# Inverse roots by a seed, a scaled Newton step and a third-order step, in 24 short VectorE chains of a graph and expert kernel

## The reference

```python
def _layernorm(x, axis=-1, eps=1e-05):
    m = jnp.mean(x, axis=axis, keepdims=True)
    v = jnp.var(x, axis=axis, keepdims=True)
    return (x - m) / jnp.sqrt(v + eps)
...
    x = x + _L0_gnn_ref(_layernorm(x, axis=-1), adj, L0_gnn_Wq, L0_gnn_Wk)
    x = x + _L0_ffn_ref(_layernorm(x, axis=-1)[None], ...)[0]
    x = x + _L1_gnn_ref(_layernorm(x, axis=-1), adj, 4096, L1_gnn_W, L1_gnn_b, L1_gnn_a)
    x = x + _L1_ffn_ref(_layernorm(x, axis=-1)[None], ...)[0]
```

## Time and profile before

| what | value |
|---|---|
| time, three runs | 826.5, 825.47, 826.3 us; median 826.3 us |
| span of the profiled execution | 825.4 us; the page gives no other time for it |
| instructions in the profile | 11636 |
| TensorE busy | 724.0 us, 88% of the span, x3481 |
| VectorE busy | 576.9 us, 70%, x1717 |
| ScalarE busy | 509.5 us, 62%, x774 |
| GpSimd busy | 180.4 us, 22%, x216 |
| stages, from the timeline | prepare to 68, attend to 449, mix and project to 547, gather and route to 825 us |

### The profile page before, as it was taken

How to read it: one execution, slowest core, us unless ns; L and a number is a source line. 1 busy time by engine, 2 the same in 40 slices (tenths; PEclk the granted TensorE clock), 3 DMA queues, 4 the chain that set the end, 5 groups by cost and what they waited for, 6 DMA issues and landing times. The chain is left out here.

```text
span 825.4 us, 11636 instructions
## 1 busy us (share of the span) xinstructions
PE 724.0 (88%) x3481; PEld 425.5 (52%) x3481; DVE 576.9 (70%) x1717; ACT 509.5 (62%) x774; POOL 180.4 (22%) x216
## 2 busy tenths in 40 slices
PE   1857999999999999999993799759999999779992
PEld 1643444444444444444442699535445656568871
DVE  7875667878787887878786458964666655655546
ACT  1736888888888888888883786841323443424330
POOL 2340000000000000000000444200445456646570
PEclk9969999999999999999997799879999999969997
DMA  4206999989997888778771200040002122124008
GB/s 130 81 0 189 316 284 253 286 255 290 259 274 230 252 229 257 238 230 259 217 218 47 95 1 2 0 116 13 27 30 70 57 69 74 42 78 107 24 27 280
DMA packets 97934, 121.92 MB, mean 148 GB/s; under 512 B 8510, under 2 KB 76355, under 8 KB 97616
## 3 DMA queue, kind: packets, MB, share of 16 engines
q1 hardware_dynamic: 93840, 113.72, 47.7%
q0 software_dynamic: 4032, 7.47, 2.8%
HBM read 87.47 MB, written 34.60 MB: 148 GB/s over the span
## 5 line engine op out<-in xcount | busy, mean ns | idle before, releaser
L562 DVE SCALAR_TENSOR_TENSOR probs<-adj,probs 128x1024 f32<-128x1024 int32 x128 | 156.7, 1224 | 77.5 <-ACT probs L535 68.4
L485 PE MATMUL ps<-x,qT 128*128 128x512 f16 x768 | 188.0, 382 | 3.2 <-PEq L203 3.2
L535 ACT ACTIVATE probs<-ps 128x1024 f32<-128x1024 f32 x128 | 130.9, 1023 | 51.1 <-PE ps L485 51.1
L546 ACT ACTIVATE mask<-probs 128x1024 fp8e4<-128x1024 f32 x128 | 134.0, 1047 | 0.0
L497 PE MATMUL ps<-probs,v 128*128 128x512 f32 x256 | 130.7, 592 | 0.0
L1462 PE MATMUL ps<-mask,parts 128*128 128x512 fp8e4 x512 | 119.7, 384 | 8.4 <-DVE parts L1829 8.4
L485 PEld LDWEIGHTS ps<-x,qT 128*128 128x128 f16 x768 | 75.5, 98 | 94.8 <-issue 5.6
L568 DVE TENSOR_TENSOR p_lo<-probs,p_hi 128x512 f16<-128x512 f32 x128 | 87.5, 684 | 0.1
L785 POOL MEMSET hT<- 128x128 f32 x1 | 0.2, 204 | 378.9 <-POOLq L438 378.9
L1462 PEld LDWEIGHTS ps<-mask,parts 128*128 128x128 f16 x512 | 50.1, 100 | 61.1 <-DVE parts L1829 8.5
L1789 POOL DMA_INDIRECT mixed_spill<-mask x70 | 68.8, 983 | 54.8 <-issue 28.2
(11 more groups left out here) (303 smaller groups left out, 1032.6 us busy)
## 6 DMA issues: line engine op xcount, KB each, us to landing
adj<-in_adj SPq DMA_DIRECT2D x128, 512.0 KB, 4.4
sorted_rows_spill<-blank SPq DMA_DIRECT2D x32, 528.0 KB
sorted_rows_spill<-blank SPq DMA_DIRECT2D x14, 330.0 KB
mask<-sorted_rows_spill SPq DMA_DIRECT2D x35, 132.0 KB, 2.3
mask<-mixed_spill SPq DMA_DIRECT2D x7, 512.0 KB, 7.8
mask<-in_x SPq DMA_DIRECT2D x4, 512.0 KB, 6.2
feat_spill<-mask SPq DMA_DIRECT2D x8, 256.0 KB, 2.0
x_feat<-in_x SPq DMA_DIRECT2D x8, 256.0 KB, 4.3
```

What stands on the lines that cost most here:

```text
L485: ins = nc.tensor.matmul(out, qT[:, q_half, j], kT[:, c, k_half * GROUP:(k_half + 1) * GROUP], start=(n == 0), stop=(n == 2))
L535: nc.scalar.activation(probs[:, k % RING, :], ps[:, b:b + 2, :].rearrange("p b n -> p (b n)"), ACT.Exp, scale=1.0 / QK_SCALE ** 2).then_in ...
L546: nc.scalar.activation(mask[:, k * W:(k + 1) * W], probs[:, k % RING, :], ACT.Sign, saturate=False).then_inc(mask_kept, 1)
L562: nc.vector.scalar_tensor_tensor(out=probs[:, k % RING, :], in0=adj[:, k % LOADS, :], scalar=0.0, in1=probs[:, k % RING, :], op0=ALU.is_gt ...
```

## The change

Each inverse root is computed in another way, from the negative variance. Epsilon and the scales of the results are taken into constants of instructions that are there anyway. Helper functions:

```diff
     me, mo, ve, vo = (stats[:, :, i] for i in (1, 4, 2, 5))
     ch.mark(nc.vector.tensor_tensor(mean, me, mo, ALU.add))
     ch.mark(nc.vector.tensor_tensor(t0, me, mo, ALU.subtract))
-    ch.link(nc.vector.tensor_tensor(t1, ve, vo, ALU.add))
-    ch.mark(nc.vector.tensor_scalar(mean, mean, 0.5, None, ALU.mult))
+    ch.link(nc.vector.scalar_tensor_tensor(out=t1, in0=ve, scalar=D * LN_EPS, in1=vo, op0=ALU.add, op1=ALU.add))
+    ch.mark(nc.vector.scalar_tensor_tensor(out=mean, in0=mean, scalar=-0.5, in1=mean, op0=ALU.mult, op1=ALU.add))
     ch.link(nc.vector.scalar_tensor_tensor(out=t0, in0=t0, scalar=0.25, in1=t0, op0=ALU.mult, op1=ALU.mult))
-    ch.link(nc.vector.scalar_tensor_tensor(out=var, in0=t1, scalar=1.0 / D, in1=t0, op0=ALU.mult, op1=ALU.add))
-
-
-def seed_root(nc, ch, y, v, t1):
-
-    ch.mark(nc.vector.tensor_scalar(y.bitcast(I32), v.bitcast(I32), -0.5, float(0x5F3759DF), ALU.mult, ALU.add))
-    ch.link(nc.vector.tensor_scalar(t1, v, -0.5, None, ALU.mult))
-
-
-def refine_root(nc, ch, y, t0, t1):
-
-    ch.link(nc.vector.tensor_tensor(t0, t1, y, ALU.mult))
-    ch.link(nc.vector.tensor_tensor(t0, t0, y, ALU.mult))
-    ch.link(nc.vector.scalar_tensor_tensor(out=y, in0=t0, scalar=1.5, in1=y, op0=ALU.add, op1=ALU.mult))
-
-
-def inverse_root(nc, ch, y, v, t0, t1):
-
-    seed_root(nc, ch, y, v, t1)
-    for _ in range(3):
-        refine_root(nc, ch, y, t0, t1)
+    ch.link(nc.vector.scalar_tensor_tensor(out=var, in0=t1, scalar=-1.0 / D, in1=t0, op0=ALU.mult, op1=ALU.subtract))
+
+
+def first_root(nc, ch, y, v, t0):
+
+
+    ch.link(nc.vector.tensor_scalar(y.bitcast(I32), v.bitcast(I32), -0.5, float(0x5F3759DF - 0x40000000), ALU.mult, ALU.add))
+    ch.link(nc.vector.tensor_tensor(t0, y, y, ALU.mult))
+    ch.link(nc.vector.tensor_tensor(t0, v, t0, ALU.mult))
+    ch.link(nc.vector.scalar_tensor_tensor(out=y, in0=t0, scalar=3.0, in1=y, op0=ALU.add, op1=ALU.mult))
+
+
+def last_root(nc, ch, y, v, t0, scale=1.0):
+
+
+    a, s = 0.5 * 1.000875, 0.375 * 0.5 * 1.000875 * scale
+    r = math.sqrt(s)
+    ch.link(nc.vector.scalar_tensor_tensor(out=t0, in0=y, scalar=-a * a * r, in1=y, op0=ALU.mult, op1=ALU.mult))
+    ch.link(nc.vector.tensor_tensor(t0, v, t0, ALU.mult))
+    ch.link(nc.vector.scalar_tensor_tensor(out=t0, in0=t0, scalar=-10.0 / 3.0 * r, in1=t0, op0=ALU.add, op1=ALU.mult))
+    ch.link(nc.vector.scalar_tensor_tensor(out=y, in0=t0, scalar=5.0 * s, in1=y, op0=ALU.add, op1=ALU.mult))
+
+
+def inverse_root(nc, ch, y, v, t0, scale=1.0):
+
+    first_root(nc, ch, y, v, t0)
+    last_root(nc, ch, y, v, t0, scale)
```

Stage 1, statistics and norms:

```diff
                 row_statistics(nc, ch, stats, mean[:, :], var[:, :], t0[:, :], t1[:, :])
-                ch.link(nc.vector.tensor_scalar(var[:, :], var[:, :], LN_EPS, None, ALU.add))
-                inverse_root(nc, ch, rstd[:, :], var[:, :], t0[:, :], t1[:, :])
-
-                ch.link(nc.vector.tensor_scalar(rstd[:, :], rstd[:, :], V_SCALE, None, ALU.mult))
+                inverse_root(nc, ch, rstd[:, :], var[:, :], t0[:, :], V_SCALE)
...
-                ch.link(nc.vector.tensor_scalar(ss[:, :], ss[:, :], 1e-8 * V_SCALE ** 2, None, ALU.max))
-                inverse_root(nc, ch, rnorm[:, :], ss[:, :], t2[:, :], t3[:, :])
-                nc.vector.tensor_scalar(rnorm[:, :], rnorm[:, :], QK_SCALE, None, ALU.mult).then_inc(norms_ready, 1)
-                dve.wait_ge(norms_ready, 1)
+                ch.link(nc.vector.tensor_scalar(ss[:, :], ss[:, :], 1e-8 * V_SCALE ** 2, -1.0, ALU.max, ALU.mult))
+                inverse_root(nc, ch, rnorm[:, :], ss[:, :], t2[:, :], QK_SCALE)
+                dve.sem_inc(norms_ready, 1)
```

Stage 2, the pieces of an ending (stages 3 and 4 drop their epsilon instruction, L928 and L1857, in the same way; ENDING goes from 33 to 29 and STEPS from 18 to 14):

```diff
                         row_statistics(nc, ch, sb["stats"][:, c * SUB:(c + 1) * SUB, :], mean, var, t0, t1)
-                        ch.link(nc.vector.tensor_scalar(var, var, LN_EPS, None, ALU.add))
 
                     def first_roots():
-                        seed_root(nc, ch, rstd, var, t1)
-                        refine_root(nc, ch, rstd, t0, t1)
+                        first_root(nc, ch, rstd, var, t0)
 
                     def last_roots():
-                        refine_root(nc, ch, rstd, t0, t1)
-                        refine_root(nc, ch, rstd, t0, t1)
+                        last_root(nc, ch, rstd, var, t0)
```

More of the change, by code:

```diff
@@ L164, in prepare @@
         mean, var, rstd, t0, t1 = (small(n, [P, TILES]) for n in ("mean0", "var0", "rstd0", "t00", "t01"))
-        ss, rnorm, t2, t3 = (small(n, [P, 2 * TILES]) for n in ("ss", "rnorm", "t02", "t03"))
+        ss, rnorm, t2 = (small(n, [P, 2 * TILES]) for n in ("ss", "rnorm", "t02"))
         hi, lo = sb["qT"][:, 0, :], sb["qT"][:, 1, :]
@@ L407, in attend @@
         TURN_STEP = 1
-        ENDING = 33
+        ENDING = 29
         adj = buf("adj", [P, LOADS, W], I32)
@@ L708, in mix_and_project @@
         CHAINS = (1, 2, 2, 1, 1, 1)
-        STEPS = 18
+        STEPS = 14
         BY_DVE = 3
@@ L927, in scale @@
                     row_statistics(nc, pc, stats[:, tiles, :], m, v, s0, s1)
-                    pc.link(nc.vector.tensor_scalar(v, v, LN_EPS, None, ALU.add))
-                    inverse_root(nc, pc, y, v, s0, s1)
+                    inverse_root(nc, pc, y, v, s0)
                     assert pc.n == STEPS
@@ L1856, in measure @@
                     row_statistics(nc, ch, sb["stats"][:, tiles, :], mean[:, tiles], var[:, tiles], t0[:, tiles], t1[:, tiles])
-                    ch.link(nc.vector.tensor_scalar(var[:, tiles], var[:, tiles], LN_EPS, None, ALU.add))
-                    inverse_root(nc, ch, rstd[:, tiles], var[:, tiles], t0[:, tiles], t1[:, tiles])
+                    inverse_root(nc, ch, rstd[:, tiles], var[:, tiles], t0[:, tiles])
                     nc.vector.scalar_tensor_tensor(out=shift[:, tiles], in0=mean[:, tiles], scalar=-1.0, in1=rstd[:, tiles],
```

## The result

The kernel after takes 820.97 us (median of 15 runs, 819.0 to 825.13), against 826.49 us for the kernel before beside it (15 runs). The ratio is 0.993, 95% interval 0.9921 to 0.9939: 5.8 us less, between 5.0 and 6.5. The forecast was 820.8 us, the sum of its terms 5.55 us.

What follows compares the result with a forecast made beforehand. TensorE is busy most of the span, so VectorE's small chains count only where an engine waits behind them. Terms 0.98 + 0.80 + 0.67 + 1.3 + 1.8 = 5.55 us off the 826.3 us median gave 820.8 us, range 818.6 to 823.6.

Steps and rivals of the forecast that it cites:

- First statistics chain: Row statistics at the start, 32 columns wide: every engine waits behind them, so all 0.98 us saved counts.
- Norms: Bare 64-column chain of the products' norms: saves 0.86 us, less GpSimd's release by a separate increment, giving 0.80 us.
- Eighth ending: Last ending of the attention, with no other work beside it: the whole chain saving counts, 0.67 us.
- Seven covered endings: Attention endings beside TensorE's attention steps: worth nothing; uncovered, up to 0.67 us each, 4.7 us together.
- FFN stage: Six chains taking turns with ScalarE, GpSimd and TensorE: 1.3 us gained, bounds 0.2 and 2.2 us.
- The cap: FFN stage: an addition behind chain three cannot pass TensorE's last products, so VectorE gains only some 0.2 us there.
- the term of chain five: FFN stage: GpSimd 1.1 us earlier, plus 0.67 saved, minus 0.5 behind the stall, lets ScalarE start 1.3 us earlier.
- Routed stage: TensorE's wait for the choice of experts in chunks one to four shrinks, 1.8 us; the other four chunks give nothing.
- GpSimd did not take the FFN gain: Rival, FFN stage: chains four and five caught for a whole GpSimd product each, 0.2 us gain, 821.9 us; chance 0.13.
- the stalls did not vanish: Rival, FFN stage: the mean's new form escapes stalls beside GpSimd, 2.0 us more gain, 818.8 us; chance 0.10.
- the stages' starts did not swallow the bare chains: Rival, attention and FFN starts: transfers set them, so only 1 us is gained, 825.3 us; chance 0.06.
- The slower rival: Expert stage: shifted waits keep TensorE at its low clock 16 us longer, losing 8 us, 828.8 us; chance 0.03.

Runs made afterwards that it cites:

- b1: Kernel before with four more linked products in each of the eight routed-stage chains (the ballast): 828.2 us, ratio 1.0028.
- s3_ffn: Kernel before with the change only in the six chains of the FFN stage: 823.58 us, ratio 0.9966.
- c1_release: Kernel after, with the last instruction of the norms' root incrementing GpSimd's semaphore itself instead of a separate increment: 820.77 us, ratio to before 0.9933.
- b2_cover: Kernel after without the third-order step in the first seven attention endings: 819.91 us, ratio to before 0.9921.

## Why the prediction was right

**The whole.** The five terms that can be read in the traces sum to about what was timed. By medians over the traces without and with a stage's change: start 46.42 and 45.41, norms 3.55 and 2.75, ending 9.06 and 8.39, FFN 2 28.42 and 26.82, chunks (without b1 and the three with the moved choice) 160.77 and 158.93. That is 1.01 + 0.80 + 0.67 + 1.60 + 1.84 = 5.92 us, or 5.79 with the norms as they reach TensorE (0.67); timed 5.8, predicted 5.55. That it agrees to 0.1 us is in part luck, since four columns are left out and move by more: from the trace of before to that of after the attention grew by 1.24 us while FFN 1, rest and end fell by 1.01, 0.69 and 0.17. The terms stand because each was found again by itself, not because of the sum.

**First statistics chain**: predicted 0.98, measured 1.01 by the column, whose traces scatter by 0.8 to 1.1 us, and 1.04 by the distance from the first statistic to the first normalized row (medians 3.91 and 2.87 us). The two profiles alone would say more. The kernel before reaches the first normalized row at 16.16 and after at 14.71, 1.45 us apart, but the six other kernels with unchanged code there reached it at 15.75 to 15.83. In the profile of before the halving of the mean in the first chain took longer than anywhere else, while GpSimd ran its own short preparations; the cause was not tested. So 0.3 to 0.4 of the 1.45 us is not the change's. Its row before, and the same in s3_ffn:

```profile
12.12 0.87 DVE L79 TENSOR_SCALAR mean<-mean 128x32 f32<-128x32 f32 x1
```

```profile
12.45 0.18 DVE L79 TENSOR_SCALAR mean<-mean 128x32 f32<-128x32 f32 x1
```

**Norms**: predicted 0.80, measured 0.80 at GpSimd's start but 0.67 at TensorE's first turn, where it counts. The chain itself lost 0.85 us, as in c1_release (0.86 forecast). The term that was too small is the release: 0.06 us was allowed for it, from a row of another place, and it costs VectorE 0.17 and TensorE 0.18 us. That the forecast holds at GpSimd's start, where the release cost 0.05, is luck. The first scaled product on VectorE came 2.22 us behind the seed and not 2.0.

**Eighth ending**: predicted 0.67, measured 0.67; that a linked step costs 0.20 and an unlinked one 0.07 us, whatever its form, was right. The prediction set this against "VectorE: DVE Perf Modes" of the Trainium skill (section "The DRAIN you can't avoid"), and by its reading a chain would have saved 0.80 us. But the sentence it quotes speaks of semaphores behind the instructions. The old seed (L86) adds to a semaphore as well, through `mark`, and cost 0.07 us: what costs the other 0.13 us is the wait for it. So the trace refutes the 0.80 and not the quoted sentence.

**Seven covered endings**: predicted nothing; shown by b2_cover and by the 317.70 us that don't change.

**FFN stage**: predicted 1.3, measured 1.6, inside its bounds. The cap and both stalls came as described: against the stage's gate product, the capped addition came 0.21 us sooner (0.2 predicted), GpSimd's product beside chain four 0.90 (0.8), and chain four ended 1.20 sooner (1.2). Too small was the term of chain five, "1.1 + 0.67 - 0.5": I let chain five start less early than GpSimd's product, so that more of it would run behind the stall. It started at 522.27 instead of 525.31 (start of its first addition), 3.04 us earlier, and GpSimd's product 2.97 us earlier, so it was caught at the same instruction (the fourth) and nothing was to be subtracted. ScalarE's release came 529.60 - 525.93 = 3.67 us earlier, 1.83 more than the stage's gate product (1.84). Of these, 1.6 us arrived at the end of the stage. So the forecast is only 0.3 us off because a loss behind chain five, which it didn't have, offset half of that error.

**Routed stage**: predicted 1.8, measured 1.84 by the column and 1.8 to 2.1 by the four distances. The value was a choice between 1.3 and 2.7, so hitting it this closely is luck; which chains count is not. The waits of chunks one to four are gone and those of five to seven stand; the ballast shows the same split from the other side. Each of the four chunks gave 0.35 to 0.59 us of the 0.67 that its chain lost, since the chain stopped being late before it was through. In the column of the rest rows nothing was taken up; in the last column something may have been, as said above.

**Rivals.** GpSimd did not take the FFN gain (FFN 2 fell by 1.6 us); the routed stage gave its part; the stalls did not vanish, since the two-input form at L80 took 1.17 us beside GpSimd just as the old halving did; the stages' starts did not swallow the bare chains on the median (the column of the attention has 389.55 us in the seven traces without the change in the first stage and 389.56 in the seven with it, with a scatter of 1.5 us). The slower rival named a mechanism that is there, at the wrong size: behind the wait TensorE is at 0.50, and how long it stays there differs, but by 1.5 us of time and not by 8. Against the prediction, the wait ahead of that stage did not stay the same: it was 5.07 us before and 5.58 after.

## What to carry to other kernels

Count the instructions that a change takes away only where an engine stands still behind them: of VectorE's 15.5 us less, 5.8 arrived, and most pieces could be read beforehand from one wait each. When a chain of small instructions is late in some rounds of a loop and not in others, look at what is late in the others: here it was the order of issue on the same engine, and changing it gave another 2.0 us in the traces (3.6 to 3.9 by time, in four runs each). For gains under half a percent cut many traces at the same instructions and compare piece by piece, with the cuts close around the changed code: the norms, the ending and the distances between chunks agreed to 0.1 us or so where whole times disagreed by 1 to 2, while longer pieces (the start, the attention, FFN 1, the end) scattered by 1 to 1.7 us themselves.

## What the runs showed of the hardware

- Behind waits of 3.6 to 6.8 us TensorE runs for a while at the granted clock of 0.50, and the moment at which it rises differs between traces with the same code there and TensorE fully busy: 0.50 or up to 0.70 over the first 5 us behind the rest rows, worth 1.5 us, and 0.55 to 0.97 over the stretch of 3 to 6 us behind the start of the FFN stage, worth 1.0 us. At the rest rows the higher clock came with the shorter waits (4.2 to 4.8 us against 5.0 to 6.8); at the FFN stage nothing was found that decides it.
- A wait with a separate increment behind a linked chain held VectorE for 0.17 us, the start of its reader GpSimd for 0.05 us and TensorE, which waits for GpSimd's first product, for 0.18 us more than an increment by the last instruction.
- VectorE instructions of 128x4 start 0.07 us apart when the first only increments a semaphore, and 0.20 us apart when the second also waits for it.
- A two-input scalar_tensor_tensor of 128x8 stalled beside GpSimd's product for as long as the tensor_scalar form had (1.17 us against 1.13), at 0.17 us when alone.
